# Post-norm block with a banded mix matrix: rounded w1 in four places, products by kind, and the second pair of x ahead of the bits

## The reference

```
attn = (w1^T w2^T) * sparse_mask                  # "mix matrix", 1024 x 1024, nonzero near the diagonal
y    = gelu(x @ attn + b2)
x1   = layernorm(x + y)
W    = lut4[o, code(o, i)]                        # code: 4 bit planes packed in int32 words
z    = x1 @ W^T + bias                            # tokens of large norm would use an 8-bit table
out  = layernorm(x1 + z)
```

## Time and profile before

| | us |
|---|---|
| median of three runs | 314.76 |
| the profiled execution | 314.7 |
| its span, first to last instruction | 312.7 |
| PE busy | 298.3 |
| DVE busy | 202.1 |
| ACT busy | 191.3 |
| POOL busy | 128.0 |
| mean granted clock of PE | 0.989 of full |

### The profile page before, as it was taken

The page is one execution under the profiler, slowest core; times in us unless marked ns, Lnnn a source line. Parts: engine busy times, 40 slices in busy tenths (PEclk is TensorE's granted clock), DMA queues, the critical chain, the costliest instruction groups (busy, mean ns, idle before and its releaser), DMA issues.

```text
span 312.7 us, 5059 instructions
## 1 busy us (share of the span) xinstructions
PE 298.3 (95%) x1907; PEld 268.1 (86%) x1907; DVE 202.1 (65%) x327; ACT 191.3 (61%) x257; POOL 128.0 (41%) x182
## 2 busy tenths in 40 slices
PE   7998999999999999999999999999999999999970
PEld 2878978888878999999999999999998878878860
DVE  0179859975995799997988877452245345342461
ACT  1067289987989499995999996936143452313110
POOL 3000031423143099998989899000033333322220
PEclk9999999999999999999999999999999999999995
DMA  7999969999997411110101111117327785443232
GB/s 220 345 372 386 373 179 273 249 257 251 161 175 134 78 44 35 48 39 19 35 20 66 36 52 48 37 50 224 98 89 245 236 259 212 168 168 124 88 125 77
DMA packets 29519, 47.66 MB, mean 152 GB/s; under 512 B 2608, under 2 KB 14768, under 8 KB 29488
## 3 DMA queue, kind: packets, MB, share of 16 engines
q1 hardware_dynamic: 24992, 38.61, 36.3%
q0 software_dynamic: 4352, 8.39, 15.3%
q10 hardware_dynamic: 144, 0.26, 0.2%
HBM read 34.67 MB, written 12.58 MB: 151 GB/s over the span
## 4 chain that ended last, share of the span: by engine, by line
PE 86%; DVE 3%; SPq 3%; DMA 2%; ACT 1%; issue 1%; POOL 1%; POOLq 0%; ACTq 0%; DVEq 0%
PE acc L445 19%; PE acc L443 19%; PE acc L444 19%; PE acc L399 7%; PE acc L401 6%; PE acc L400 6%; PE acc L428 5%; PE acc L380 3%; DMA w_raw<-in_w2b 2%; PE acc L407 2%; SPq L231 1%; DVE w_lo L825 1%; DVE w_lo L818 1%; SPq L225 1%; SPq L221 1%
## 5 line engine op out<-in xcount | busy, mean ns | idle before, releaser
L443 PE MATMUL acc<-lin,zz 128*128 128x256 f32 (+2 forms) x424 | 130.1, 307 | 0.0
L445 PE MATMUL acc<-lin,zz 128*128 128x256 f32 (+2 forms) x424 | 129.8, 306 | 0.0
L444 PE MATMUL acc<-lin,zz 128*128 128x256 f32 (+2 forms) x424 | 129.6, 306 | 0.0
L444 PEld LDWEIGHTS acc<-lin,zz 128*128 128x128 f32 x424 | 80.2, 189 | 4.0
L445 PEld LDWEIGHTS acc<-lin,zz 128*128 128x128 f32 x424 | 80.1, 189 | 4.1
L443 PEld LDWEIGHTS acc<-lin,zz 128*128 128x128 f32 x424 | 80.0, 189 | 4.1
L616 ACT ACTIVATE leaf<-planes,lut,flip 128x1024 f32<-128x1024 uint8 x56 | 67.2, 1234 | 3.3 <-DVE leaf L879 1.9
L1270 POOL DMA_DIRECT2D z<-in_xt x16 | 19.6, 1227 | 77.9 <-ACT z L597 77.9
L879 DVE COPY_PREDICATED leaf<-planes,leaf 128x1024 f32<-128x1024 uint8 x32 | 43.7, 1366 | 11.3 <-ACT leaf L616 10.8
L734 ACT ACTIVATE junk<-rows,cols 128x1024 bf16<-128x1024 f32 x15 | 17.2, 1150 | 39.1 <-POOL cols L1244 39.0
L1003 DVE TENSOR_SCALAR rows<-rows,cols 128x1024 f32<-128x1024 f32 x15 | 12.2, 812 | 37.9 <-POOL cols L1251 37.9
(11 more groups left out here) (97 smaller groups left out, 423.4 us busy)
## 6 DMA issues: line engine op xcount, KB each, us to landing
z<-in_xt SPq DMA_DIRECT2D x16, 512.0 KB, 9.0
z<-in_xt POOLq DMA_DIRECT2D x16, 512.0 KB, 8.6
out_rows<-rows SPq DMA_DIRECT2D x15, 512.0 KB, 2.7
w_stage<-in_w1b SPq DMA_DIRECT2D x8, 512.0 KB, 6.5
out_rows<-parts SPq DMA_DIRECT2D x32, 128.0 KB, 1.9
rows<-out_rows SPq DMA_DIRECT2D x16, 256.0 KB, 3.0
w_raw<-in_w2b SPq DMA_DIRECT2D x5, 512.0 KB, 6.9
w_stage<-in_w2b SPq DMA_DIRECT2D x3, 512.0 KB, 7.8
```

What stands on the lines that cost most here:

```text
L443: nc.tensor.matmul(bank, hi, w_hi, start=k == 0, stop=False)
L444: nc.tensor.matmul(bank, hi, w_lo, start=False, stop=False)
L445: last = nc.tensor.matmul(bank, lo, w_hi, start=False, stop=k == KB - 1)
```

## The change

`w1_hi` gets four places, so ACT no longer waits before it rounds w1(6) and w1(7). `w1_lo` gets four places too and lies at the address of `w1_stage`: DVE subtracts in place. `make_mix(b)` for b of 4 to 7 now does all eight hi*hi products first, waiting only for the rounded parts, then eight with w1_lo after a wait for it, then eight with w2_lo after a wait for that. Since w1_lo now lies where x of group 1 comes, SP waits for all eight mix rows before that load. x pair 1 is loaded ahead of `q_low`. On DVE the last mask and rest of the mix matrix come before the first bit planes and before the rest of x pair 2. The step tables move single decode steps: two of them two units earlier in stage 3, one from tile 8 to tile 9 of the first pass, one from the second pass to the end of the first, and some by one tile within the second pass.

```diff
-    UNIT_STEPS = [0, 1, 0, 1, 0, 2, 2, 1, 1, 1, 1, 0, 0, 1, 1, 0, 0, 1, 0, 1, 3, 2, ...
+    UNIT_STEPS = [0, 1, 0, 1, 0, 2, 2, 1, 1, 1, 1, 0, 0, 1, 1, 1, 0, 1, 0, 0, 3, 2, ...
...
-        w1_hi = at("w1_hi", 128, [2, KB, P], f32r)
-        w1_lo = at("w1_lo", 136, [2, KB, P], f32r)
+        w1_hi = at("w1_hi", 128, [STAGES, KB, P], f32r)
+        w1_lo = at("w1_lo", 16, [STAGES, KB, P], f32r)
...
                 if g == 1:
-                    sp.wait_ge(w1_lo_made, KB - FULL)
-                if g == 2:
                     sp.wait_ge(mix_made, KB)
...
-                    if g == 0 and r == 0:
+                    if g == 0 and r == 1:
                         sp.dma_start(q_low[:, :, :, :],
...
-                products = ((w1_hi, w2_hi), (w1_hi, w2_lo), (w1_lo, w2_hi))
+                products = ((w1_hi, w2_hi), (w1_lo, w2_hi), (w1_hi, w2_lo))
...
-                    pe.wait_ge(w1_lo_made, b - FULL + 1)
-                    pe.wait_ge(w2_lo_made, slabs - SPLIT)
-                    for d in range(KB):
-                        for n in range(3):
-                            w1_part, w2_part = products[n]
-                            last = nc.tensor.matmul(acc[:, b % 2, 0:end - first], w1_part[:, b % 2, d, :],
+                    pe.wait_ge(w1_hi_made, b - FULL + 1)
+                    pe.wait_ge(w2_hi_made, slabs - SPLIT)
+                    for n in range(3):
+                        if n == 1:
+                            pe.wait_ge(w1_lo_made, b - FULL + 1)
+                        if n == 2:
+                            pe.wait_ge(w2_lo_made, slabs - SPLIT)
+                        w1_part, w2_part = products[n]
+                        for d in range(KB):
+                            last = nc.tensor.matmul(acc[:, b % 2, 0:end - first], w1_part[:, b % STAGES, d, :],
                                                     w2_part[:, d, first:end], start=(d, n) == (0, 0),
...
             def make_w1_hi(b):
                 act.wait_ge(raw_loaded[b % STAGES], 64 if b == STAGES else 48)
-                if b >= FULL + 2:
-                    act.wait_ge(mix_made, b - 1)
...
             make_mix_lo(KB - 2)
+            mask_mix(KB - 1)
+            make_mix_lo(KB - 1)
             make_planes(0)
-            mask_mix(KB - 1)
             make_x_lo(0, 2)
-            make_mix_lo(KB - 1)
             make_x_lo(0, 3)
```

More of the change, by code:

```diff
@@ L53, in post_ln_block @@
     DECODE_ALL = DECODE * KB + len(STARTS)
-    UNIT_STEPS = [0, 1, 0, 1, 0, 2, 2, 1, 1, 1, 1, 0, 0, 1, 1, 0, 0, 1, 0, 1, 3, 2, 1, 0, 1, 0, 0, 0, 0, 0, 0, 0]
-    FIRST_STEPS = [1, 2, 1, 2, 3, 1, 1, 2, 3, 1, 2, 3, 3, 3, 3, 0]
-    SECOND_STEPS = [1, 3, 3, 2, 3, 1, 2, 2, 1, 2, 0, 2, 3, 3, 2, 0]
+    UNIT_STEPS = [0, 1, 0, 1, 0, 2, 2, 1, 1, 1, 1, 0, 0, 1, 1, 1, 0, 1, 0, 0, 3, 2, 1, 0, 1, 0, 0, 0, 0, 0, 0, 0]
+    FIRST_STEPS = [1, 2, 1, 2, 3, 1, 1, 2, 2, 2, 2, 3, 3, 3, 3, 1]
+    SECOND_STEPS = [1, 3, 3, 1, 3, 1, 1, 2, 2, 2, 0, 2, 3, 3, 2, 0]
     ROWS_OF_1, LINEAR_OF_1 = (3, 4), (3, 6)
@@ L562, in make_w1_hi @@
                 act.wait_ge(raw_loaded[b % STAGES], 64 if b == STAGES else 48)
-                if b >= FULL + 2:
-                    act.wait_ge(mix_made, b - 1)
-                nc.scalar.activation(w1_hi[:, b % 2, :, :], w1_stage[:, b % STAGES, :, :], ACT.Copy).then_inc(w1_hi_made, 1)
+                nc.scalar.activation(w1_hi[:, b % STAGES, :, :], w1_stage[:, b % STAGES, :, :], ACT.Copy).then_inc(w1_hi_made, 1)
             def make_w2_hi(t):
@@ L817, in make_w1_lo @@
                 dve.wait_ge(w1_hi_made, b - FULL + 1)
-                nc.vector.tensor_tensor(w1_lo[:, b % 2, :, :], w1_stage[:, b % STAGES, :, :],
-                                        w1_hi[:, b % 2, :, :].bitcast(f32), ALU.subtract).then_inc(w1_lo_made, 1)
+                nc.vector.tensor_tensor(w1_lo[:, b % STAGES, :, :], w1_stage[:, b % STAGES, :, :],
+                                        w1_hi[:, b % STAGES, :, :].bitcast(f32), ALU.subtract).then_inc(w1_lo_made, 1)
             def make_w2_lo(t):
```

## The result

The changed kernel takes 312.84 us (median of four runs, 312.72 to 313.31); its ratio to the kernel before is 0.9941, 95% interval 0.9924 to 0.9958. The forecast was 313.5 with a range from 313.0 to 314.3: the sign was right, the gain of 1.9 us was outside the range, by 0.16 us at the median. The profiled execution took 312.73 us.

A forecast was written before the change was run, and what follows sets the result against it. The prediction took PE as the bound, working in 95% of the span. Gains of 1.08 us at the second output block and 0.23 at the later hole summed to 1.3, giving a median of 313.5 us, range 313.0 to 314.3.

The forecast's parts named there:

- the stretch from the second to the fourth block: PE's output blocks from 36.95 to 41.3 us; planes ahead of x pair 2 cost 0.2 us at most.
- the kept room of the second transpose: Row 1's transpose, before at 96.84 us: its chain waits on PE and keeps its 0.16 us of room.
- rival c: Load of x of group 1, requested 2 us later, comes late: 4.4 us lost against 1.3 won, 317.8 us; chance 0.05.
- rival b: After a wait at row 1's transpose PE loses what it won: 314.4 to 314.8 us; chance 0.13.
- sorting is free: Rows 4 to 7: the trace has no shared weight load to lose, so sorting products by kind costs nothing.
- the sum: Whole kernel: 1.08 us and 0.23 us give a gain of 1.3 us, median 313.5 us.
- gain at the second output block: PE starts mix(0, 1) at 36.95 instead of 38.03 us, behind a new 0.9 us hole: 1.08 us gained.
- the hole at 88: PE's 0.23 us hole at 88.55, behind the rest of x pair 2 of group 3, goes: 0.23 us more.
- behind the last product: End of the span after PE's last product: the forecast counted no gain there.
- Nothing of the change makes that load earlier: Load of x pair 0 stays behind the same masks and weights in SP's queue; ACT rounds it from 32.20 us.
- (d): Hole at 36.05 us is smaller because x pair 0 lands up to 2 us earlier: 312.8 us; chance 0.05.
- the change pays exactly what it takes out of PE's holes: PE is the bound, so the gain equals its removed holes, as long as ACT and DVE keep ahead.

The follow-up runs named there:

- e3: Changed kernel with the three step tables of the kernel before; ratio to the kernel before 0.9942 (0.9929 to 0.9955).
- e6: Changed kernel with the rounded w1 in two places again instead of four; ratio to the kernel before 0.9949 (0.9927 to 0.9972).
- e1: Changed kernel run again with no edit, as a control; ratio to the kernel before 0.9945 (0.9929 to 0.9961).
- e4: Changed kernel with the planes of row block 0 again ahead of the last mask on DVE; ratio to the kernel before 0.9967 (0.9954 to 0.9980).
- e13: Kernel before with x pair 0 of group 0 loaded ahead of the last two masks; ratio to the kernel before 0.9998 (0.9984 to 1.0012).
- e8: Kernel before with only x pair 1 loaded ahead of the low bits; ratio to the kernel before 0.9982 (0.9967 to 0.9996).
- e12: Changed kernel with x pair 0 of group 0 loaded ahead of the last two masks; ratio to the kernel before 0.9921 (0.9903 to 0.9938).
- e7: Kernel before with only the products by kind and their waits; ratio to the kernel before 0.9992 (0.9976 to 1.0008).
- e10: Changed kernel with x pair 1 of group 0 rounded on ACT instead of DVE; median 312.48 us, ratio to the kernel before 0.9917.
- e5: Changed kernel with the split products of rows 4 to 7 again in turn, behind both rests; ratio to the kernel before 0.9951 (0.9935 to 0.9967).
- e14: Changed kernel with x pair 1 rounded on ACT, planes behind x pair 2's rest, and x pair 0 loaded ahead of the last masks; median 312.65 us, ratio 0.9923.

## Why the forecast was off

**Right, within 0.15 us.** Row 4 at 22.8 (22.87), ACT on w1(6) at 26.3 (26.31), the end of rows 4 to 7 at 34.5 (34.63), the stretch from the second to the fourth block with the planes in it (4.35 forecast, 4.34), the kept room of the second transpose (94.90 to 95.20), no late x of group 1 (ACT takes it at 44.02 with no wait; rival c), no gain given back (rival b). That x pair 1 would then be late and a new hole take back part of what rows 4 to 7 won was right as well. That the loads of weights are per product and sorting is free: PE shows 1907 weight loads again. What the Trainium skill says in "TensorE: Matmul & The Clock Gate", section "Step-by-step: what each phase is for", that weights can be loaded once and multiplied with repeatedly, has nothing to save in this trace in either order.

**The step that failed is the sum, 1.08 + 0.23 = 1.3 us.** The mechanism held, but both of its terms were too small, and a third was taken as nothing:

| term | forecast | measured |
|---|---|---|
| gain at the second output block | 1.08 | 1.30 |
| the hole at 88 | 0.23 | 0.35 |
| behind the last product | nothing | 0.27 |
| sum | 1.3 | 1.9 |

*The second output block.* I put it at 36.95, behind a hole of 0.9 us; it stood at 36.73, behind 0.71. 0.08 us is DVE's overlap: I summed durations, where starts stand about 0.1 us closer. The other 0.14 us is the load of x pair 0, which ACT took at 32.06 instead of 32.20.

*The hole at 88.* 0.23 us was the hole; with it went the slower restart behind it, and the row was worth 0.35 (16.26 - 15.91 between the transposes; e3 gives 0.31).

*Behind the last product.* There after has the shortest tail of all sixteen profiles (9.9 us, e6 10.0, the others up to 10.4). The forecast gave it nothing, since the change does not touch what runs there. I take it for chance on those grounds, but no run shows its cause, and it is the largest of the three gaps.

**The range was too narrow because of x pair 0.** "Nothing of the change makes that load earlier" was true, but I made one fixed number of it and gave (d) one chance in twenty. In the thirteen profiles of kernels that have the same loads in front of it, ACT takes it anywhere between 31.04 and 32.91 us. The second block of the changed kernel stands 4.67 us behind that, in after, e1, e3 and e4, where PE waits for DVE's rest of x; it can't come before PE is through with its own products, at 36.02 in after. That of the kernel before does not feel an earlier landing (e13). It hangs on another load instead: its row 4 starts 2.46 us behind ACT's start on slab 5 of w2, in before (21.54 to 24.00), e8 (21.90 to 24.36) and e13 (21.84 to 24.30) alike, and ACT waits for that slab's load each time. So the change moved the bound from one load to another, and the landings of both vary.

**What was luck.** The median of 312.84 is almost the 312.8 of rival (d), but (d)'s mechanism, an earlier landing of x pair 0, gave only 0.14 us in the profile. And the ten runs of the changed program have their mean inside the range, at 313.06, and lie between 312.41 and 313.84 (before in the same rounds as e1: 314.15 to 315.17), so that the four runs fell outside it by 0.16 us is in part chance. How early the load landed in the runs without a profile can't be seen, and e12, which asks for it earlier, did not narrow the spread clearly. That the spread of the times comes from this load is therefore not shown.

**Holes of PE are not the price.** The prediction opened with "the change pays exactly what it takes out of PE's holes". e7 takes out both large holes and gains nothing: what counts is which lane ends last at each output block.

**The parts don't add.** Taken out of the changed kernel, the load order costs 0.6 us, the DVE order 0.6, the tables 0.3 (in the profile), the products by kind 0.2 to 0.5, the four places of w1_hi nothing that shows. Put into the kernel before alone, the products by kind give nothing and the load order 0.4. A lane is a chain of work, on one engine or over several, that must end before PE can go on; each part shortens one of several lanes that end within about 1 us of each other. Shortening the next one (e10) gave as much again as any part of the change.

## What to carry to other kernels

Before pricing a removed hole, list every lane that ends near it, with the instruction order of each engine, and take the latest; a part can be worth nothing alone (e7) and something beside the others (e5). When the next lane ends in a DMA, its landing may differ between runs by more than the edit is worth (here 0.85 us between two profiles of one program): take the range from that, and read edits by distances inside one profile. On DVE and ACT sum the distances of starts, not durations.

## What the runs showed of the hardware

The same 512 KB load, issued at 24.37 us behind the same transfers, landed after 7.7 us in after and 8.5 in e1. Issued 0.74 us earlier and ahead of two masks, it took 8.3 us in e12 (31.9), but 7.1 in e14 (issued at 23.98). PE's first product started between 8.11 and 9.04 us over sixteen profiles, and the same start goes with different landings of x pair 0 (8.46 with ACT's start on it at 32.06 and at 32.91). The granted clock of the stretch from 41 us on was 1.00 in after, the full 2.4 GHz level, with a hole of 0.94 us between two starts before it. In-place subtraction of w1_lo kept its 1.22 us.
